# The two nearest distances of a causal convolution, moved from fp32 to three fp32r passes over high and low parts

## What is computed

```python
def _get_kernel(log_dt, C, log_A_real, A_imag, length):
    ...
    P = dtA[:, :, None] * jnp.arange(length, dtype=jnp.float32)
    Cs = Cc * (jnp.exp(dtA) - 1.0) / A
    K = 2.0 * jnp.einsum('hn,hnl->hl', Cs, jnp.exp(P)).real
    return K
...
u_m = u * mask[:, None, :]
kernel = _get_kernel(log_dt, C, log_A_real, A_imag, Lq)
n = 2 * Lq
k_f = jnp.fft.rfft(kernel, n=n)
u_f = jnp.fft.rfft(u_m, n=n)
y = jnp.fft.irfft(u_f * k_f, n=n)[..., :Lq]
y = y + u_m * D[:, None]
return y * mask[:, None, :]
...
x = x + _L0_attn_ref(_L0_cond_ref(x, ...), Wq, Wk, Wv, Wo)
x = x + _L0_ffn_ref(_L0_cond2_ref(x, weights, condition), W_base, gate_W, A, B)
```

## Time and profile before

| | us |
|---|---|
| median of 3 runs | 876.0 (874.11 to 876.84) |
| the profiled execution | 876.56 |
| its span in the trace | 874.7 |
| first step of the convolution starts | 20.55 |
| step 4 starts | 41.14 |
| step 24 starts | 129.80 |
| convolution ends, value projection starts | 164.33 |

### The profile page before, as it was taken

How to read it: one execution, slowest core, us unless ns; L and a number is a source line. 1 busy time by engine, 2 the same in 40 slices (tenths; PEclk the granted TensorE clock), 3 DMA queues, 4 the chain that set the end, 5 groups by cost and what they waited for, 6 DMA issues and landing times.

```text
span 874.7 us, 24616 instructions
## 1 busy us (share of the span) xinstructions
PE 854.1 (98%) x10866; PEld 741.9 (85%) x10866; DVE 467.1 (53%) x898; ACT 221.4 (25%) x377; POOL 450.0 (51%) x346
## 2 busy tenths in 40 slices
PE   3999999999999999999999999999999999999998
PEld 2899999988888888887777777777779999999998
DVE  7555651122522222238887777888854755545444
ACT  4445552100000000013132333333334322211220
POOL 3344555302367555649978888877746422102220
PEclk9999999999999999999999999999999999999999
DMA  3788877413354322255534454545437211222211
GB/s 95 177 207 220 208 186 196 162 60 127 109 183 129 82 74 73 50 166 154 142 129 149 135 176 165 173 163 173 151 123 234 96 59 57 83 97 97 98 49 49
DMA packets 97339, 114.90 MB, mean 131 GB/s; under 512 B 44112, under 2 KB 66896, under 8 KB 97232
## 3 DMA queue, kind: packets, MB, share of 16 engines
q1 hardware_dynamic: 94240, 112.29, 43.1%
q10 hardware_dynamic: 2480, 0.51, 0.3%
q0 software_dynamic: 512, 0.53, 0.2%
HBM read 80.16 MB, written 33.13 MB: 130 GB/s over the span
## 4 chain that ended last, share of the span: by engine, by line
PE 93%; SPq 3%; DMA 2%; DVE 1%; issue 0%; ACT 0%
PE ps L988 25%; PE ps L1275 21%; PE ps L1597 15%; PE ps L649 8%; PE ps L1625 5%; PE ps L952 5%; PE ps L660 4%; PE ps L1231 3%; PE ps L1211 3%; PE ps L1507 2%; SPq L606 2%; DMA toep<-kpad 2%; PE ps L1642 1%; PE ps L1641 1%; DMA kpad<-ksb 1%
## 5 line engine op out<-in xcount | busy, mean ns | idle before, releaser
L1597 PE MATMUL ps<-wb_hi,xf 128*128 128x424 f32 x440 | 127.0, 356 | 0.0
L988 PE MATMUL ps<-y_hi,w_hi 128*128 128x512 f32 x320 | 125.1, 391 | 0.0
L988 PE MATMUL ps<-y_hi,w_lo 128*128 128x512 f32 x320 | 124.5, 389 | 0.0
L988 PE MATMUL ps<-y_lo,w_hi 128*128 128x512 f32 x320 | 124.5, 389 | 0.0
L1573 POOL TENSOR_TENSOR xf<-xs,xf 128x512 fp32r<-128x512 f32 x32 | 42.1, 1347 | 124.8 <-DVE xs L1561 124.8
L1275 PE MATMUL ps<-y_hi 128*128 128x512 f32 x256 | 102.9, 402 | 0.0
L1275 PE MATMUL ps<-y_hi,y_lo 128*128 128x512 f32 x256 | 100.2, 391 | 0.0
L1275 PE MATMUL ps<-y_lo,y_hi 128*128 128x512 f32 x256 | 100.1, 391 | 0.0
L649 PE MATMUL ps<-xc,toep 64*128 64x192 f32 (+4 forms) x1088 | 97.1, 330 | 2.5 <-DMA toep<-kpad 2.4
L649 PEld LDWEIGHTS ps<-xc,toep 64*128 64x128 f32 x1088 | 91.2, 187 | 6.0 <-issue 3.8
L1597 PEld LDWEIGHTS ps<-wb_hi,xf 128*128 128x128 f32 x440 | 82.7, 188 | 2.3
(11 more groups left out here) (190 smaller groups left out, 1624.3 us busy)
## 6 DMA issues: line engine op xcount, KB each, us to landing
toep<-kpad SPq DMA_DIRECT2D x124, 136.0 KB
xc<-in_dram SPq DMA_DIRECT2D x32, 256.0 KB, 4.4
q_rows<-rf SPq DMA_DIRECT2D x32, 256.0 KB, 2.8
q<-q_rows SPq DMA_DIRECT2D x16, 512.0 KB, 3.9
xr<-in_dram SPq DMA_DIRECT2D x16, 512.0 KB, 4.4
x_scratch<-xr SPq DMA_DIRECT2D x16, 512.0 KB, 3.0
x<-x_scratch SPq DMA_DIRECT2D x16, 512.0 KB, 4.3
out_dram<-x SPq DMA_DIRECT2D x15, 512.0 KB, 2.9
```

Of the source, the lines that this page charges most:

```text
L988: mm = pe.matmul(kq_bank(n), w[a][:, j, :], yt[b][:, j, g * 512:(g + 1) * 512], start=(j == 0 and a + b == 0), stop=(j == NJ - 1 and a == 1))
L1597: mm = pe.matmul(dst[:, PLAIN:], xf(i, idx, a)[:, t, :], wb(c, idx, t), start=(start and t == 0 and a + c == 0), stop=(t == 3 and a == 1), ...
```

## The change

For steps from 2 on, the four tiles of d = 0 and 1 are no longer fp32. Input and rows are split into a high part (a copy to fp32r) and a low part (the difference), and each tile takes three fp32r passes: high x high, high rows x low input, low rows x high input. The tiles stay 64 rows x 128 columns, also (0, 0) of the odd steps, which was narrow.

- ScalarE gets two copies per step, `near_hi(n + 2)`, behind `y_hi` of step n: the input (512 elements per partition) and the rows (320). Ahead of the second it waits until all rows of step n + 2 have landed.
- GpSimd gets one subtraction of 512 elements, `near_lo_x(n + 2)`, behind `y_lo` of step n.
- VectorE gets one subtraction of 320 elements, `near_lo_rows(n + 1)`, ahead of mask n.
- TensorE, even step: five wide fp32 tiles, the near tiles, the seven narrow. Odd step: the seven narrow, the five wide, the near tiles last. Ahead of the near tiles it waits for all three engines.
- The split input lives in the third slot of the weight ring of the next stage, so that the load and split of weight unit 0 are moved behind the convolution. Some parameter tiles share space with the new ones.

```diff
@@ near tiles
+        FIRST_NEAR = 2
+        NEAR = 4
+        def near_tiles(pe, n):
+            pe.wait_ge(a_near, 2 * (n - FIRST_NEAR + 1))
+            pe.wait_ge(g_near, n - FIRST_NEAR + 1)
+            pe.wait_ge(v_near, n - FIRST_NEAR + 1)
+            for d, c in TILES[:NEAR]:
+                at = d * P + (1 - c) * HALF
+                for a, b in PASSES:
+                    for r in range(2):
+                        rows = slice(r * HALF, (r + 1) * HALF)
+                        mm = pe.matmul(ps[:, 2 * (n % 3) + r, d * NB:NJ * NB], near[a][rows, n % 2, at:at + P],
+                                       xs_pair[b][rows, n % 2, 1 - c, 0:(NJ - d) * NB],
+                                       start=False, stop=True, skip_group_check=True)
+            return mm
@@ convolve
+            if n >= FIRST_NEAR and n % 2 == 0:
+                for d, c in WIDE[NEAR:]:
+                    wide(pe, n, c, d, start=((d, c) == WIDE[NEAR]), stop=True)
+                near_tiles(pe, n)
+                for d, c in NARROW:
+                    mm = narrow(pe, n, c, d, start=False, stop=True)
+            elif n >= FIRST_NEAR:
+                for d, c in NARROW:
+                    narrow(pe, n, c, d, start=((d, c) == NARROW[0]), stop=True)
+                for d, c in WIDE[NEAR:]:
+                    wide(pe, n, c, d, start=False, stop=True)
+                mm = near_tiles(pe, n)
@@ conv_masks, ahead of the mask of step n
+                if FIRST_NEAR <= n + 1 < S // 2:
+                    near_lo_rows(v, n + 1)
@@ new
+        def near_hi(act, n):
+            act.wait_ge(ld_xc[n // XH % XR], 16 * 2 * (n // XH // XR + 1))
+            act.activation(xs_pair[0][:, n % 2, :, :], xc[:, n // XH % XR, :, n % XH, :], ACT.Copy).then_inc(a_near, 1)
+            act.wait_ge(ld_toep[n % TR], rows_landed(n))
+            act.activation(near[0][:, n % 2, :], toep[:, n % TR, 0:NEAR_COLS], ACT.Copy).then_inc(a_near, 1)
+        def near_lo_x(gp, n):
+            gp.wait_ge(a_near, 2 * (n - FIRST_NEAR) + 1)
+            gp.tensor_tensor(xs_pair[1][:, n % 2, :, :], xc[:, n // XH % XR, :, n % XH, :],
+                             xs_pair[0][:, n % 2, :, :].bitcast(F32), ALU.subtract).then_inc(g_near, 1)
+        def near_lo_rows(v, n):
+            v.wait_ge(a_near, 2 * (n - FIRST_NEAR) + 2)
+            v.tensor_tensor(near[1][:, n % 2, :], toep[:, n % TR, 0:NEAR_COLS],
+                            near[0][:, n % 2, :].bitcast(F32), ALU.subtract).then_inc(v_near, 1)
@@ conv_hi, behind y_hi of step n
+                if n + FIRST_NEAR < S // 2:
+                    near_hi(act, n + FIRST_NEAR)
                 if n == 0:
                     store_kernels(act, 1)
@@ conv_lo, behind y_lo of step n
+                if n + FIRST_NEAR < S // 2:
+                    near_lo_x(gp, n + FIRST_NEAR)
-                if n == W_FIRST + 17:
-                    weight_lo(gp, 0)
```

More of the change, by code:

```diff
@@ L145, in build @@
         len_f = sb("len_f", [P, NB], F32, s1)
-        prm = sb("prm", [P, 5, S], F32, s1)
-        t64 = sb("t64", [P, 24, S], F32, s1)
+        t64 = sb("t64", [P, 6, S], F32, s1)
         d_at = sb("d_at", [P, NHG, 2], F32, s1)
@@ L155, in build @@
         ksb = sb("ksb", [P, 2, 2, GP * HB], F32, s1)
+        first = ExitStack()
+        prm = sb("prm", [P, 5, S], F32, first)
+        t64_first = sb("t64_first", [P, 18, S], F32, first)
+        first.close()
+        NEAR_COLS = 2 * P + HALF
+        near = [sb(f"near_{n}", [P, 2, NEAR_COLS], F32R, s1) for n in ("hi", "lo")]
         s1.close()
+        xs_pair = [w[:, WR - 1, :].rearrange("p (r c n) -> p r c n", r=2, c=2) for w in wsp]
         s2 = ExitStack()
@@ L297, in build @@
             "pe_conv", "v_mask", "a_yhi", "g_ylo")]
+        a_near, v_near, g_near = [signal(n) for n in (
+            "a_near", "v_near", "g_near")]
         a_whi, g_wlo, pe_unit = [signal(n) for n in (
@@ L638, in conv_loads @@
                 part, piece = divmod(n - W_FIRST + 1, W_PIECES)
-                if 0 <= part < 3:
+                if 0 <= part < 2:
                     cols = slice(piece * W_COLS, (piece + 1) * W_COLS)
-                    source = w_v[:, part * NJ * P:(part + 1) * NJ * P] if part < 2 else w_qk[0]
-                    sp.dma_start(wraw[:, part, cols], source[:, cols]).then_inc(ld_w[part // 2 * 2], 16)
+                    source = w_v[:, part * NJ * P:(part + 1) * NJ * P]
+                    sp.dma_start(wraw[:, part, cols], source[:, cols]).then_inc(ld_w[0], 16)
         def wide(pe, n, c, d, start, stop=False):
@@ L650, in wide @@
                                xc[rows, n // XH % XR, 1 - c, n % XH, 0:(NJ - d) * NB],
-                               start=start, stop=stop)
+                               start=start, stop=stop, skip_group_check=(n >= FIRST_NEAR and not start))
             return mm
@@ L799, in w_loaded @@
             s = w_slot(m).start
-            pieces = (2 * W_PIECES, 0, W_PIECES)[s]
-            whole = 0 if m <= 0 else (m - 1) // WR + 1 if s == 0 else m // WR + (s == 1)
+            pieces = (2 * W_PIECES, 0, 0)[s]
+            whole = 0 if m < 0 else (m - 1) // WR + 1 if s == 0 else m // WR + 1
             eng.wait_ge(ld_w[s], 16 * (pieces + whole))
@@ L884, in qkv_transfers @@
         def qkv_transfers(sp):
+            load_weights(sp, 0)
             load_weights(sp, 1)
@@ L1003, in qkv_hi @@
             act.wait_ge(g_ylo, S // 2)
+            weight_hi(act, 0)
             for n in range(4 * NU):
@@ L1075, in qkv_rope_sin @@
         def qkv_rope_sin(gp):
+            weight_lo(gp, 0)
             for n in range(4 * NU):
```

10 lines of the change are left out of this document (4 added, 6 removed).

## The result

| | us, median (lowest to highest), runs |
|---|---|
| kernel before, measured beside it | 876.42 (874.11 to 879.12), 4 |
| changed kernel | **900.27** (898.21 to 905.85), 4 |
| ratio | **1.0272**, 95% interval 1.0241 to 1.0303 |
| profiled execution before / after | 876.56 / 898.84, spans 874.7 / 897.0 |

A forecast was written before the change was run, and what follows sets the result against it. The prediction took TensorE to bound the convolution, with loads close behind. Start +4.5, five groups +8.3 and end -1.3 sum to +11.5 on the profiled 876.56, or 888.1; 0.56 above the median, so forecast 887.5, range 877 to 893.

The forecast's parts named there:

- the wait behind the sine block: At steps 4m + 3 TensorE would wait about 3 us for GpSimd's low input, made behind ScalarE's sine block.
- The sign: The changed kernel would be slower, +11.5 us; slower by over 0.3% was given a chance of 0.82.
- rival of serial passes: fp32r passes of 64 rows don't run side by side, near tiles take 2.7 us, kernel some 916; chance 0.06.
- 84 ns a load: Earlier trace's 32 fp32 weight loads in 2.68 us, cited against the 107 ns per load that would make passes serial.
- covered case: Rival: ScalarE's and GpSimd's new work is ready in time and loads set the pace; 869 or 864 us, chance 0.11.
- What TensorE gains: Near tiles in fp32r passes save TensorE 0.4 us a step, leaving 3.85 to 3.9.
- 1.36: Near tiles' time per step in us after the change: 6 passes at 0.12 and 6 at 0.107, instead of 1.75.
- The sine block, five groups at 19.4: Steps 4 to 23: each group of four steps takes 19.4 us instead of 17.7, together +8.3.
- The start, +4.5: Row copies delay ScalarE's kernel store by 2.9 us, so step 4 starts at 45.65, not 41.14: +4.5 (4.0 to 5.0).
- The end, -1.3: Steps 24 to 31, with no sine block, take 33.2 us instead of 34.5: -1.3 (bounds -3.2 and -0.4).
- At nothing: Loading, copying and splitting weight unit 0 behind the convolution costs nothing, covered by 44 us of value tiles.
- The range: 877 to 893 us, to hold 8 in 10; all terms at their high ends give 893.

The follow-up runs named there:

- e1: Changed kernel with near passes reading a resting tile of constants, the added copies, subtractions and waits left out; 876.59 us, ratio 0.9998 to the kernel before.
- e9: e1 with each load of rows from step 4 on bringing 64 columns of a piece instead of 544; 868.91 us, ratio 0.9891 to the kernel before.
- e10: Kernel before the change, with loads of rows from step 4 on shortened to 64 columns of a piece; 873.20 us, ratio 0.9959 to the kernel before.
- e6: Changed kernel with VectorE making the low rows of steps 4m + 2 ahead of the last part of the phases; 899.52 us, ratio 1.0242 to before.
- e12: Changed kernel whole, with loads of rows from step 4 on shortened to 64 columns of a piece; 900.82 us, ratio 1.0275 to the kernel before.
- e14: Changed kernel with the value weights' copy (ScalarE) and subtractions (GpSimd) moved from steps 15 and 19 to 24, 25 and 28; 894.20 us, ratio 1.0173 to before.
- e4: Changed kernel without GpSimd's low input and TensorE's wait for it, third pass reading the high input; 889.69 us, ratio 1.0136 to the kernel before.

## Why the prediction missed

The step that failed is the wait behind the sine block: it was worked out for GpSimd and ScalarE with VectorE's phases at their old length, and the runs show VectorE's phases stretched from 4.4 to 6.5 us a group by GpSimd's added instruction, and TensorE waiting for what stands behind them. By parts, the miss of 10.3 us is 5.2 in the five groups, 4.1 in the last eight steps and 1.1 at the start.

**What held.** The sign, and the reason for it: the passes run side by side (a pair every 0.12 and 0.11 us, so the rival of serial passes falls; the 84 ns a load that spoke against it did not, since the 32 loads of the earlier trace rows run two by two, 0.007 us apart, and a single one takes 0.18 to 0.19), and the added work isn't covered. The covered case (864 to 869) is refuted twice: the work isn't covered, and e1 shows that with all of it covered the kernel would be at 876.6.

**What TensorE gains.** The step falls by 0.21 (e9 against e10) to 0.24 (e1), not 0.4, and stays at 3.98 instead of 3.85. Both terms of that difference were mis-sized. The spacing behind "1.36" is right, but the first pair is followed after 0.20 and the tile behind the near tiles starts late too:

```profile
77.38 0.39 PE L690 MATMUL ps<-w_hi,near_hi 64*128 64x256 f32 x2 [1.55 <-DVE near_lo L808]
77.57 0.31 PE L690 MATMUL ps<-w_lo,near_hi 64*128 64x256 f32 x2
...
78.94 2.10 PE L669 MATMUL ps<-xc,toep 64*64 64x128 f32 x100
```

From the first pair to the next tile it is 1.56 here, ahead of a narrow tile, and 1.43 to 1.46 ahead of the small matmuls or a wide tile. The fp32 tiles that they replace take 1.62 in an even step of e10 and 1.75 in an odd one, 1.69 in the mean: the 1.82 ns per column, a mean over all wide tiles, is too much for the four largest. At 0.13 a step for 28 steps this is at most 3.6 us of the miss, less where TensorE waits anyway.

**The sine block, five groups at 19.4.** Wrong in what binds. The working followed ScalarE and GpSimd to step 4m + 3 and called VectorE's a "smaller wait". VectorE's is the one that binds at step 4m + 2, since the phases grew from 4.4 to 6.5 us beside a busier GpSimd, and GpSimd's, named by the prediction, is level with it: e6 takes away the first and meets the second. The earlier trace rows gave the price of GpSimd's instructions, and the working had no term for what they do to a neighbour. Its premise, a group that starts with the landing of rows at 8.6 to 9.2 a pair, fell with e12. The three groups without value weights took 18.9, 20.1 and 19.9, near the 19.4, for another reason; that is luck. The two with them took 21.9 and 21.5, which is most of the 5.2. The working left out that GpSimd's 2.5 us for value weights stand ahead of and beside their phases. Moved away they give 6.1 us (e14) by the medians; how much of it lies in these two groups is not shown.

**The start, +4.5.** It came to +5.6. The wait for GpSimd at step 3 is there and TensorE entered its near tiles at 43.15, not 43.6. What was missing is the half clock behind it: 2.7 for the near tiles instead of 1.36.

**The end, -1.3.** It came to +2.8: 37.3 us instead of 33.2. Two stops, at 163.1 and 180.4, idle 2.8 of these 4.1, and the step of 3.98 instead of 3.85 makes 1.0.

**At nothing.** Weight unit 0 costs nothing, as said: behind the projection's start the two profiled executions differ by 22.3 - 21.8 = 0.5.

**The range.** It took each term to its own high end (893) but had no term for slowed neighbours, for the clock and for stops. The stops idle 6.5 us, the half clock behind step 3 takes 1.3 in the near tiles alone, and the slowed phases are part of e4's 10.6; these overlap, and no run gives each its price.

## What to carry to other kernels

Cost added work on the engine that gets it and on the neighbour that it slows: here an instruction of 1.3 us a step on a half-idle GpSimd cost 10.6 us, and it made VectorE's unchanged phases a quarter longer (26.1 to 32.4 us). For each new wait write down what stands ahead of it on each of the engines that feed it, in program order; if two of them are late, curing one (e6) shows the other and gains nothing. And measure the gain with the work left out first: e1 would have said at once that the best case was a tie, since stops of 5.3 us had taken the gain.

## What the hardware showed that was not expected

TensorE stops for 0.7 to 2.1 us in the midst of tiles for which everything lies ready, at positions whole multiples of 256 instructions apart, and goes on 1.2 to 1.7 us behind the landing of a 16 KB packet of the instruction queue; with short loads all of these stops are gone in e9, and two of five stay in e12. At TensorE's wait of 4.3 us the clock is 1.2 GHz for 6.8 us, 5.0 of them behind the wait; the one of 2.58 at step 18 is followed by 3.4, the one of 2.52 at step 22 and the three of 1.05 to 1.55 by none: a wait can go on costing behind its end, and not by a rule that these rows would show. And one VectorE instruction of the phases, at the last three of the eight, takes 410 to 426 ns alone and 1015 to 1491 beside a GpSimd instruction in the changed kernel, with nothing changed in it.
